# Attention scores of a decoder layer: which query half the vector engine masks, and a new written-out order

## The reference

```python
q = (x @ wq).reshape(Bq, Tq, N_KV, N_REP, HEAD_DIM)          # 8 heads of 128, 2 groups
k = einsum('bkhl,ld->bkhd', x @ wk_down, wk_up)               # latent size 32
scores = where(causal, einsum(q, k) * scale, min)             # 256 x 256 per head
x = x + softmax(scores) @ v ... @ wo
x = x + cross_attention(layernorm(x), ctx) then relu MLP      # 16 heads of 16, 77 context rows
x = x + ffn(layernorm(x))                                     # ternary weights, int8 activations, gelu, 1024 wide
```

## Time and profile before

| | |
|---|---|
| median of 3 runs | 303.56 us |
| the profiled execution, whole | 303.98 us |
| its span, first to last instruction | 302.2 us |
| TensorE (PE) busy | 286.0 us, 95% |
| ScalarE (ACT) | 240.6 us, 80% |
| VectorE (DVE) | 227.3 us, 75% |
| GpSimd (POOL) | 173.5 us, 57% |
| weight loads (PEld), beside the matmuls | 230.9 us, 76% |
| mean granted clock of TensorE | 0.994 |

### The profile page before, as it was taken

How to read it: one execution, slowest core, us unless ns; L and a number is a source line. 1 busy time by engine, 2 the same in 40 slices (tenths; PEclk the granted TensorE clock), 3 DMA queues, 4 the chain that set the end, 5 groups by cost and what they waited for, 6 DMA issues and landing times.

```text
span 302.2 us, 9763 instructions
## 1 busy us (share of the span) xinstructions
PE 286.0 (95%) x3470; PEld 230.9 (76%) x3470; DVE 227.3 (75%) x423; ACT 240.6 (80%) x642; POOL 173.5 (57%) x368
## 2 busy tenths in 40 slices
PE   8996999999999999999999999999999999999573
PEld 7674787778888877888787897888888789787242
DVE  1144756896886866998786698786897899999992
ACT  3669988875389478999996788999997689896681
POOL 8234087163344880578978540448458885875843
PEclk9999999999999999999999999999999999999989
DMA  7999100000000000000000100000001000010112
GB/s 208 341 365 347 64 3 1 2 0 5 0 3 3 2 2 2 3 0 3 0 4 2 35 4 2 4 2 20 0 4 37 1 4 17 2 38 4 35 35 72
DMA packets 12103, 12.69 MB, mean 42 GB/s; under 512 B 1684, under 2 KB 11288, under 8 KB 12056
## 3 DMA queue, kind: packets, MB, share of 16 engines
q1 hardware_dynamic: 10648, 11.40, 11.7%
q10 hardware_dynamic: 1408, 0.67, 0.8%
HBM read 9.96 MB, written 2.10 MB: 40 GB/s over the span
## 4 chain that ended last, share of the span: by engine, by line
PE 75%; DVE 8%; DMA 5%; issue 3%; POOL 3%; SPq 3%; ACT 1%; DVEq 0%; POOLq 0%; ACTq 0%
PE bank L2139 9%; PE bank L2148 8%; PE bank L1945 7%; PE bank L2027 7%; PE bank L1951 5%; PE bank L2130 5%; PE bank L2168 4%; PE quad L2112 4%; PE quad L2006 4%; PE quad L2089 4%; PE bank L2039 4%; DMA xres<-in_x 3%; PE bank L2187 3%; PE bank L1939 2%; DMA out<-f_o 2%
## 5 line engine op out<-in xcount | busy, mean ns | idle before, releaser
L962 ACT ACTIVATE c_p<-quad 77x512 f32<-77x512 f32 x64 | 34.1, 594 | 6.2 <-PE quad L2116 5.9
L2139 PE MATMUL bank<-c_y,xw_s 128*128 128x128 f32 x256 | 31.9, 278 | 0.2 <-DVE c_y L1518 0.2
L2148 PE MATMUL bank<-xw_s,c_h 128*128 128x256 f32 x128 | 30.7, 383 | 0.3 <-ACT c_h L971 0.3
L916 ACT ACTIVATE a_sB<-quad,a_nmB 128x256 f32<-128x256 f32 x64 | 29.6, 490 | 1.5 <-DVE a_nmB L1452 1.5
L2139 PEld LDWEIGHTS bank<-c_y,xw_s 128*128 128x128 f32 x256 | 30.0, 192 | 0.8 <-DVE c_y L1518 0.4
L925 ACT ACTIVATE a_p<-bank 128x512 f32<-128x512 f32 x48 | 26.4, 601 | 3.6 <-PE bank L2027 3.2
L1499 DVE TENSOR_REDUCE c_nm<-quad 128x16 f32<-128x1232 f32 x16 | 23.0, 1438 | 6.9 <-PE quad L2089 6.8
L2148 PEld LDWEIGHTS bank<-xw_s,c_h 128*128 128x128 f32 x128 | 23.5, 190 | 4.1 <-ACT c_h L971 0.5
L916 ACT ACTIVATE a_sA<-a_mA,a_nmA 128x128 f32<-128x128 f32 x64 | 25.3, 407 | 0.1
L552 POOL TENSOR_SCALAR a_xn<-xres,a_mv,a_rs 128x256 f32<-128x256 f32 x16 | 20.0, 1254 | 6.5 <-PE bank L1939 6.0
L1452 DVE TENSOR_REDUCE a_nmB<-quad 128x8 f32<-128x2048 f32 x8 | 18.3, 2290 | 6.8 <-PE quad L2011 6.8
(11 more groups left out here) (167 smaller groups left out, 801.5 us busy)
## 6 DMA issues: line engine op xcount, KB each, us to landing
out<-f_o SPq DMA_DIRECT2D x16, 128.0 KB, 1.7
xres<-in_x SPq DMA_DIRECT2D x1, 1536.0 KB, 10.0
c_p<-in_wqT SPq DMA_DIRECT2D x2, 512.0 KB, 6.7
c_p<-in_wo SPq DMA_DIRECT2D x1, 1024.0 KB, 9.4
f_h<-in_fw1T SPq DMA_DIRECT2D x1, 1024.0 KB, 12.3
fw_t<-in_fw2T SPq DMA_DIRECT2D x1, 1024.0 KB, 11.3
xw_s<-in_xw SPq DMA_DIRECT2D x2, 512.0 KB, 9.8
fb_s<-in_fb SPq DMA_DIRECT2D x1, 512.0 KB, 6.8
```

Of the source, the lines that this page charges most:

```text
L916: nc.scalar.activation(s[:, r, c, :], scores, ACT.Exp, bias=nm[:, r, c:c + 1], accum_out=a_sum[:, qt, c, r:r + 1]).then_inc(sa.sem["act"], 1)
L962: nc.scalar.activation(c_p[0:M, :, qt * P:(qt + 1) * P].rearrange("p (c j g) t -> p c j g t", c=KC, g=Q2)[:, :, j, :, :], quad[0:M, j, :]. ...
L2139: last = mm(bank("xm", f"w1{t}", i)[:, m * P:(m + 1) * P], xw1_s[:, c, m * P:(m + 1) * P], c_y[:, t, c, :], start=c == 0, stop=c == KC - 1)
L2148: last = mm(bank("xm", f"w2{t}", i)[:, 0:D], c_h[:, m, t * P:(t + 1) * P], xw2_s[:, m, :], start=m == 0, stop=m == MC - 1)
```

## The change

VectorE now masks part B and TensorE masks part A in the banks. Since B's copy in SBUF is 8 KB per partition in place of A's 4 KB, the float32 feed-forward weight `fw2` shares memory with the scratch tiles `f_sq` and `f_hq`; so batch 0's f2 ssq and hq wait for the last conversion of that weight. All engines' orders are written anew.

```diff
 QUAD_EMPTIED = {
-    ("sa", "suA"): ("dve", ("mkA",)),
-    ("sa", "suB"): ("act", ("exB01", "exB11", "exB21", "exB31")),
+    ("sa", "suA"): ("act", ("exA01", "exA11", "exA21", "exA31")),
+    ("sa", "suB"): ("dve", ("mkB",)),
...
-MASKED_BY_VECTOR = ("A",)
+MASKED_BY_VECTOR = ("B",)
...
-        f_sq = sb("f_sq", [P, TT, FH], BF16)
-        f_hq = sb("f_hq", [P, TT, FH], F16)
+        f_w = sb("f_w", [P, TT, FH])
+        f_sq = f_w[:, 0, :].bitcast(BF16).rearrange("p (t h) -> p t h", t=TT)
+        f_hq = f_w[:, 1, :].bitcast(F16).rearrange("p (t h) -> p t h", t=TT)
...
-        fw2_t = sb("fw2_t", [P, FC, D])
-        fw2_s = fw2_t[:, :, :]
+        fw2_s = f_w[:, :, :].rearrange("p t h -> p (t h)").rearrange("p (c d) -> p c d", d=D)
...
-            pro_ones()
             sp_rstd(0)
             sp_norm(0)
+            pro_ones()
...
             def f2_ssq(i, t):
...
+                if i == 0:
+                    act.wait_ge(*pro.after("pool", "t2", 0))
...
             def f2_hq(i, t):
                 dve.wait_ge(*f2.after("act", f"ssq{t}", i))
+                if i == 0:
+                    dve.wait_ge(*pro.after("pool", "t2", 0))
...
             for n in range(WARM):
                 mm(quad[:, 0, 0:P], onesq[:, :], onesq[:, :], start=True, stop=True)
-            pro_v(2)
-            pro_k(0)
-            pro_k(2)
-            pro_k(3)
+            pro_wq(0)
             sp_xT(0)
-            pro_wq(0)
             pro_wq(1)
```

More of the change, by code:

```diff
@@ new lines, in _ @@
+            xs_exp(4, 1, 2)
+            sp_xT(7)
+            xs_exp(4, 1, 1)
+            xs_exp(4, 1, 0)
+            f1_pre(2)
+            xm_relu(3, 1)
+            f1_gelu(2, 1)
+            xp_xT(5)
+            sp_k(7)
+            sa_copy(6, "A", 0)
+            f2_ssq(2, 1)
+            xp_q(5)
+            f2_hT(1, 0)
+            f1_gelu(2, 0)
+            sa_exp(6, "B", 2)
+            sa_exp(6, "B", 0)
+            sp_q(7)
+            sa_exp(6, "B", 1)
+            sa_exp(6, "B", 3)
@@ new lines, in _ @@
+            xs_exp(6, 0, 1)
+            xs_exp(6, 0, 3)
+            xs_mT(6, 1)
+            f2_pre(7)
+            xs_exp(6, 0, 0)
+            xs_exp(6, 0, 2)
+            f1_qT(4, 0)
+            xm_relu(5, 1)
+            f2_hT(3, 0)
+            xs_exp(6, 1, 3)
+            xs_exp(6, 1, 1)
+            xs_exp(6, 1, 0)
+            xs_exp(6, 1, 2)
+            xp_xT(7)
+            f1_pre(4)
+            f1_gelu(4, 0)
+            xp_q(7)
+            f1_gelu(4, 1)
+            f2_ssq(4, 0)
@@ new lines, in _ @@
+            f1_h(0, 2)
+            sa_mask(4, "B")
+            so_y(3, 1)
+            xm_resid(1, 0)
+            sa_max(4, "B")
+            so_y(3, 0)
+            f2_hmax(0, 0)
+            sa_max(5, "A")
+            sa_inv(4, "A")
+            xo_T(2, 1)
+            so_resid(3)
+            xm_resid(1, 1)
+            f2_hq(0, 0)
+            sa_inv(4, "B")
+            xp_ln(3)
+            xo_y(2, 1)
+            f1_ln(1, 0)
+            so_y(4, 0)
+            f1_ln(1, 1)
+            so_y(4, 1)
@@ L1793, in _ @@
+            xo_T(3, 0)
+            f1_h(1, 3)
+            xs_max(4, 1)
+            f1_ln(2, 1)
+            xo_y(3, 0)
+            f2_out(0, 0)
+            f2_hmax(1, 0)
+            f1_q(2, 0)
+            f2_out(0, 1)
+            f2_hmax(1, 1)
+            xo_T(3, 1)
+            f1_q(2, 1)
+            so_y(5, 0)
+            so_y(5, 1)
+            sa_max(6, "A")
+            so_resid(5)
+            f2_hq(1, 0)
+            xp_ln(5)
+            xo_y(3, 1)
+            f2_hq(1, 1)
             xm_resid(3, 0)
+            xo_T(4, 0)
@@ new lines, in _ @@
+            xm_w2(1, 1)
+            sa_tr(4, "B", 3)
+            sa_tr(4, "B", 0)
+            sa_tr(4, "B", 2)
+            xm_w1(2, 0)
+            so_rd(4)
+            so_pv(4, 0)
+            so_pv(4, 1)
+            sa_scores(5, "B")
+            xm_w1(2, 1)
+            xp_xT(3)
+            sa_tr(5, "A", 0)
+            so_wo(4)
+            xp_q(3)
+            sa_tr(5, "A", 1)
+            sp_q(6)
+            f2_hT(0, 0)
+            f1_qT(1, 1)
+            xs_scores(3, 0)
+            sp_v(5)
@@ new lines, in _ @@
+            xm_w2(2, 0)
+            xp_xT(4)
+            xs_scores(3, 1)
+            f1_qT(1, 0)
+            xs_mT(3, 0)
+            sa_tr(5, "B", 2)
+            sa_tr(5, "B", 1)
+            f1_l1(1, 1)
+            f1_l1(1, 0)
+            xs_shift(3, 0)
+            xp_q(4)
+            f1_l1(1, 2)
+            xm_w2(2, 1)
+            xs_scores(4, 0)
+            xo_pv(3, 0)
+            sa_tr(5, "B", 0)
+            xs_mT(3, 1)
+            f1_l1(1, 3)
+            xs_scores(4, 1)
+            sa_tr(5, "B", 3)
@@ L2509, in _ @@
-            xm_w1(5, 1)
+            f2_l2(2, 1)
             xm_w2(5, 0)
             xs_mT(6, 1)
-            xm_w2(5, 1)
+            f1_qT(4, 0)
+            xm_w1(5, 1)
+            f2_hT(3, 0)
+            f1_l1(4, 3)
+            xs_shift(6, 1)
+            xo_pv(6, 0)
             f1_l1(4, 0)
```

1685 lines of the change are left out of this document (788 added, 897 removed).

## The result

The changed kernel takes 309.69 us (median of 4 runs, 308.95 to 310.78) against 303.4 us for the kernel before in the same job: a ratio of 1.0224, 95% interval 1.0199 to 1.0249. Run again later beside other kernels it came to 309.39 us and a ratio of 1.0210 (1.0191 to 1.0228). The forecast of 305.6 us had the sign right and the size wrong: 6.3 us were lost beside the kernel before of the same job (6.1 from the 303.56 us that the forecast started from), not 2.0, and the time lies above the range. The profiled execution took 309.51 us with a span of 307.6 us, 5.4 us more than the span before.

What follows compares the result with a forecast made beforehand. TensorE was taken as the bound, solid in the middle, so start and tail decide. Terms 1.4 + 1.1 + 0.5 - 1.0 = +2.0 us on the 303.56 us median gave 305.6 us, range 302.2 to 308.5.

Steps and rivals of the forecast that it cites:

- TensorE's work at 0: All batches: identity-by-mask matmuls move from second to first query half, 32 of 275 ns before and after; 0 us.
- The start, +1.4: Start: TensorE idles after warm-ups until wqT lands, 4.7 us lost, 3.3 taken back before 30 us; +1.4 us.
- The clock, +1.1: Behind the start's pause: TensorE's clock may fall, running wq0, xT0 and wq1 at half rate; +1.1 us, bounds 0 and +1.9.
- VectorE's copy, 1.2 us each and 0 on the path: Body: eight added 128x1024 copies from PSUM, 9.6 us in all, fit into VectorE's 44.6 us without work; 0 us.
- ScalarE, 0: Exponentials: first half now reads PSUM, second SBUF; shifts of 28 ns each, down and up, cancel; 0 us.
- The banks, +0.5: Four score banks: first half frees them 3.3 us later, second 3.8 sooner; new waits +0.5 us, bounds -0.9 and +3.
- The tail, -1.0: Tail: one maximum fewer on VectorE ahead of the last batch's quantised rows; -1.0 us, bounds -2.7 and +1.
- A: Rival: as summed, slower by the start; 304.2 to 307.5 us, chance 0.34.
- D: Rival: VectorE bounds the body, half of eight copies cost 1.2 us each; 310 us, chance 0.12.
- B: Rival: faster, VectorE's shorter tail queue saves 1.2 us and TensorE's kept clock 1.7; 302.1 or 301.2 us, chance 0.24.
- C: Rival: no measurable change, tail's gain cancels start's loss and the clock stays up; 304.0 us, chance 0.16.
- E: Rival: low clock covers all of wq0, xT0 and wq1, tail has its own spell, no gain; 306.9 us, chance 0.14.

Runs made afterwards that it cites:

- putting the steps back: Changed kernel with weight steps v2, k0, k2 and k3 back ahead of wq0 on TensorE, with their copies on other engines: 306.82 us, ratio 1.0139.
- taken apart: Changed kernel's order with the old masking (TensorE masks the second half, VectorE the first, no copy): 363.29 us, ratio 1.1957.
- all repairs: Changed kernel with four weight steps back ahead of wq0, two GpSimd additions later, ScalarE's q copy (batch 2) and an exponential reordered: 305.97 us, ratio 1.0099.

## Why the prediction was wrong in size

- **What bounds it; TensorE's work at 0.** Right. TensorE's busy time is the same (286.2 us), and in the solid middle there was only something to lose.
- **The start, +1.4.** Right. wqT's first half let TensorE go at 10.51 us against 10.8 forecast (10.29 to 11.75 over the profiles, so the near hit is partly luck); of the pause, all but 1.2 us was made up before 30 us. That 1.2 and the slower clock's 1.9 make 3.1, half a us from the 2.6 us that putting the steps back gives back.
- **The clock, +1.1.** Right in kind, low in size: it took about 1.9 us, the upper bound of that term. From 10.5 to 15.4 us the clock was 0.50, longer than the three steps on which the estimate stopped. The rule of the Trainium skill (TensorE: Matmul & The Clock Gate, Part 1) that was set against the rows, that an idle array falls back to the lower level, described this case; the view that only the tail shows such spells did not.
- **VectorE's copy, 1.2 us each and 0 on the path.** The duration was right (1220 ns, so no doubled rate out of PSUM). The zero holds in the new order, to the 1.2 us of that interval (309.72 us without seven of them), but the argument for it, that VectorE has 44.6 us without work in the body, was wrong: by the same argument the old order would hide such a copy, and there it costs 6.5 us. VectorE's total rose by 6.4 us only, to 233.7 where I forecast 236.9. Part of what lacks is in rows: f_c took 356 ns in place of 451, the product c_u 549 in place of 606. The rest I haven't located; it isn't the additions on GpSimd, beside which six instructions were lengthened before and five after.
- **ScalarE, 0.** Its total fell by 2.3 us. The exponentials took 388 and 512 ns, near what the relu and the SBUF row gave.
- **The banks, +0.5.** This term failed first. TensorE's idle time between 30 and 260 us went from 0.5 to 3.3 us, and some 1.8 us of the increase are real waits, the rest missing records. They aren't for the score banks: what the term looked at went well. What it left out is the rest of a new order: copies behind exponentials on ScalarE, normalised rows late from GpSimd at 54 and 218 us, quantised rows late from VectorE at 102, behind a product that took 1.36 us beside a GpSimd addition. That ScalarE's queue would matter was written down, and then priced at half a microsecond.
- **The tail, -1.0.** This term failed worst. It counted only what the shorter queue of VectorE saves behind the last w2 step (the second matmul of the cross-attention's MLP), and there the kernel is indeed 1.1 us shorter (27.3 us before, 26.2 after). Nothing was put down for the stretch ahead of that step, where VectorE feeds TensorE too: between 260 us and that step TensorE's idle time rose from 0.5 to 2.4 us, most of it the one stall of 1.68 us. From 260 us on it is 1.2 us more, where 1.0 less was forecast. And the reason given for the gain doesn't hold in the old order, where moving the maximum saves nothing; that the 1.1 us came is no proof of it.
- **The sum.** Start and clock came to 2.6 us against 2.5 forecast, the body to 1.8 against 0.5, the tail to 1.2 against -1.0: together 5.6 against 2.0. Measured were 6.3. Some tenths of the rest lie outside the span: what a run takes beyond it is 1.8 us in every kernel of the old order and 1.8 to 2.4 us on average in those of the new one. Why is open.
- **The rivals.** A's own span ended at 307.5 us. D gave 310 us (by its own terms 310.4), the right time for the wrong reason: it had TensorE wait in the body for VectorE with its long piece of copy, mask and maximum. No such wait is in the trace, and leaving seven copies out saved nothing. What D had seen rightly is that VectorE has little room, in the old order. B and C fell with the tail. E was right about the clock's full price.

What stays open: the changed kernel with all repairs is still 1.0% (0.8 to 1.2) slower than the kernel before. Its trace has 1.4 us of idle time between 30 and 60 us and 2.1 between 60 and 260 (about 1 of it missing records), in gaps of 0.1 to 0.6 us behind ScalarE, GpSimd and VectorE in turn, and 0.7 us more than the kernel before from 260 us on. The gaps that were attacked closed and opened again in part, so I take them for the price of this order as a whole; that is argued and not shown.

## What to carry to other kernels

An engine's idle share doesn't say that it can take more: eight copies on VectorE cost 6.5 us when added to one order; in the other, seven of them cost nothing that can be measured and eight more cost 3.5 us. Only experiments that add or remove the load told these apart. Where one step frees a shared buffer and the order is written around that moment, the two are one design: taken apart they gave 363 us. A stall is worth its length only if what comes next has its inputs; moved away alone, the holes at 23 and 268 us and in the tail came back within a few steps, while the idle start with its slow clock gave back 2.6 of about 3.1 us. And look past the place of a repair, up to the next wait that grew: the one at 268 us came back at 280.
